# Turning the normed rows beside the attention: TensorE transposes against VectorE blocks placed by DMA

## What is computed

```python
x = x + xattn(layernorm(x), ctx, Wq, Wk, Wv, Wo)
#   q = xn @ Wq.T * 16**-0.5; k = ctx @ Wk.T; v = ctx @ Wv.T     (16 heads)
#   o = sigmoid(q k^T) v ; o @ Wo.T
x = x + ffn(layernorm(x), gate_w, Wg, Wu, Wd, Ws_g, Ws_u, Ws_d)
#   scores = softmax(h @ gate_w.T); each of 16 experts takes its top 64 rows of a batch
#   expert: (gelu(t @ Wg.T) * (t @ Wu.T)) @ Wd.T, weighted and added; shared expert on all rows
```

## Time and profile before

| | us |
|---|---|
| median of 3 runs | 1478.99 (1475.84 to 1479.41) |
| the profiled execution's own time | 1478.48 |
| its span, first to last instruction | 1476.7 |
| TensorE matmul busy | 1407.8 (95%) |
| ScalarE busy | 942.0 (64%) |
| VectorE busy | 654.3 (44%) |
| mean granted TensorE clock | 0.975 of full |

### The profile page before, as it was taken

One profiled execution on the slowest core, in us unless ns is written; L12 is line 12 of the kernel. 1 busy time (PEld: TensorE's weight loads), 2 busy tenths in 40 slices (PEclk: granted clock), 3 DMA queues, 4 the chain that ended last, 5 costly groups with the idle time before them and its releaser, 6 DMA issues.

```text
span 1476.7 us, 22519 instructions
## 1 busy us (share of the span) xinstructions
PE 1407.8 (95%) x9046; PEld 789.5 (53%) x9046; DVE 654.3 (44%) x1305; ACT 942.0 (64%) x1061; POOL 209.7 (14%) x171
## 2 busy tenths in 40 slices
PE   3897999999999999999999999999999999999996
PEld 2443434434434444443443443333788888888885
DVE  4334225325314423432632431220447677777773
ACT  0475867787787788778778778998232344334341
POOL 0000000000000000000000000020000236666664
PEclk9898999999999999999999999999899999999998
DMA  4463496286467548539647834841344446666643
GB/s 153 151 136 106 110 147 150 94 133 143 140 105 127 144 110 135 150 109 131 143 136 102 131 118 96 111 143 48 142 139 133 125 146 155 160 153 143 147 99 41
DMA packets 101145, 187.74 MB, mean 127 GB/s; under 512 B 17200, under 2 KB 51504, under 8 KB 101040
## 3 DMA queue, kind: packets, MB, share of 16 engines
q1 hardware_dynamic: 84192, 155.06, 45.4%
q0 software_dynamic: 16000, 29.91, 10.0%
q10 hardware_dynamic: 848, 1.31, 0.3%
HBM read 122.24 MB, written 64.00 MB: 126 GB/s over the span
## 4 chain that ended last, share of the span: by engine, by line
PE 89%; DMA 3%; DVE 3%; ACT 2%; issue 1%; SPq 1%; POOL 0%; POOLq 0%; DVEq 0%
PE acc L1185 26%; PE score L1225 17%; PE score L1169 17%; PE score L1240 9%; PE misc L1083 6%; PE misc L1096 6%; PE misc L1119 2%; PE misc L1104 2%; ACT probs L600 2%; PE misc L1128 1%; DMA key_scr<-key_parts 1%; PE misc L1111 1%; SPq L348 1%; DMA keys<-key_scr 1%; PE acc L1252 0%
## 5 line engine op out<-in xcount | busy, mean ns | idle before, releaser
L600 ACT ACTIVATE probs<-score 128x1024 f32<-128x1024 f32 (+1 forms) x832 | 780.8, 1048 | 207.3 <-PE score L1169 206.5
L1185 PE MATMUL acc<-probs,values 128*32 128x512 f32 (+1 forms) x3328 | 448.1, 611 | 5.7 <-ACT probs L600 3.1
L1169 PE MATMUL score<-queries,keys 48*128 48x512 f32 (+1 forms) x1664 | 317.1, 454 | 3.0 <-DMA keys<-key_scr 3.0
L1169 PEld LDWEIGHTS score<-queries,keys 48*128 48x128 f32 (+1 forms) x1664 | 127.4, 182 | 255.8 <-ACT probs L600 204.3
L609 ACT ACTIVATE gelu<-score 128x512 f32<-128x512 f32 x96 | 57.1, 595 | 214.6 <-PE score L1225 212.5
L1185 PEld LDWEIGHTS acc<-probs,values 128*32 128x32 f32 (+1 forms) x3328 | 66.4, 108 | 153.1 <-issue 131.1
L511 POOL DMA_DIRECT2D ctx_raw<-ctx_t x32 | 23.4, 732 | 810.5 <-DVE ctx_lo L686 809.4
L692 DVE CAST key_parts<-misc 128x512 fp32r<-128x512 f32 (+1 forms) x64 | 36.8, 575 | 215.8 <-PE misc L1083 201.7
L1225 PE MATMUL score<-tok_hi,gu_hi 128*128 128x512 f32 x384 | 120.1, 394 | 0.0
L1225 PE MATMUL score<-tok_lo,gu_hi 128*128 128x512 f32 x384 | 119.4, 392 | 0.0
L1225 PE MATMUL score<-tok_hi,gu_lo 128*128 128x512 f32 x384 | 119.3, 392 | 0.0
(11 more groups left out here) (128 smaller groups left out, 1457.2 us busy)
## 6 DMA issues: line engine op xcount, KB each, us to landing
keys<-key_scr SPq DMA_DIRECT2D x180, 200.2 KB, 10.2
key_scr<-key_parts SPq DMA_DIRECT2D x48, 512.0 KB, 4.5
gu_raw<-w_gu SPq DMA_DIRECT2D x17, 1024.0 KB, 6.5
ctx_raw<-ctx_t POOLq DMA_DIRECT2D x24, 512.0 KB, 4.3
queries<-query_scr SPq DMA_DIRECT2D x180, 64.0 KB, 3.0
d_raw<-w_d SPq DMA_DIRECT2D x17, 512.0 KB, 8.9
query_scr<-query_parts SPq DMA_DIRECT2D x15, 512.0 KB, 2.9
xn<-x SPq DMA_DIRECT2D x8, 512.0 KB, 3.8
```

Of the source, the lines that this page charges most:

```text
L600: act.activation(probs[0:rows, n % RING, 2 * pair:2 * pair + 2, :], score[k % 3][0:rows, :, :], ACT.Sigmoid, scale=SCALE).then_inc(probs_d ...
L1169: mm = pe.matmul(score[k % 3][0:rows, g, :], keys[quarter % KEY_RING][of, pair, P * st:P * st + rows], queries[half][of, e, pair, :], star ...
L1185: mm = pe.matmul(acc[32 * c:32 * (c + 1), :], values[b % 2][0:rows, st, half, c, :], probs[0:rows, n % RING, c, :], start=(st == 0), stop= ...
```

## The change

The T tasks of batches 1 to 7 and the N tasks of batches 0 to 6 leave the slots; each tensor is transposed in four steps instead:

1. `turn_rows` (VectorE): one instruction transposes every 32 by 32 block of the 128 x 1024 tensor into the new buffer `row_blocks`. There is one such buffer for both tensors, so a turn first waits until the placing before it has landed.
2. `place_rows` (SyncE): 16 DMAs from SBUF to SBUF, 32 partitions with two runs of 512 B each, put the blocks at their partitions, back into `norm` or `xn`. For `norm` they wait for the store of the rows (`store_norm`).
3. `split_rows` (VectorE): four instructions, cast and subtraction for each of the two halves, read SBUF and write `nt_hi` and `nt_lo`, putting the rows in order.
4. TensorE's query product waits for the split of T, its gate product for that of N (`wait_rows`).

The remaining tasks are given other slots (`at_quad`), and the slots of the layernorm pieces move by one. Some small tensors of the second stage move to its part of SBUF, which makes room for the buffer and changes no instruction.

```diff
+TURN = 32
+BLOCKS = P // TURN
+PLACE_DMAS = 16 * BLOCKS ** 2
...
-        at_quad = (12, 14, 16, 18, 20, 22, 24, 26, 28, 29, 31, 33, 35, 37, 39, 41, 43, 45, 47)
+        at_quad = (12, 14, 16, 18, 21, 23, 25, 27, 29, 34, 36, 38, 40, 42, 44, 46, 48)
     else:
-        tasks = {4: ("O", b - 1, 0), 6: ("O", b - 1, 1), 20: ("N", b - 1, 0), 21: ("N", b - 1, 1),
-                 23: ("G", b - 1)}
-        at_quad = (0, 2, 8, 10, 12, 14, 16, 18, 25, 26, 28, 30, 32, 34, 36, 38, 40, 42, 44)
+        tasks = {5: ("O", b - 1, 0), 7: ("O", b - 1, 1), 24: ("G", b - 1)}
+        at_quad = (0, 2, 10, 12, 14, 17, 19, 22, 26, 29, 31, 34, 36, 38, 41, 43, 46)
     if b + 1 < B:
-        c = b + 1
-        names = [("K", c, 0, 0), ("K", c, 1, 0), ("V", c, 0, 0), ("V", c, 0, 1),
-                 ("K", c, 0, 1), ("K", c, 1, 1), ("V", c, 1, 0), ("V", c, 1, 1),
-                 ("T", c, 0), ("T", c, 1), ("Q", c, 0), ("Q", c, 1),
-                 ("K", c, 0, 2), ("K", c, 1, 2), ("V", c, 2, 0), ("V", c, 2, 1),
-                 ("K", c, 0, 3), ("K", c, 1, 3), ("V", c, 3, 0)]
         tasks.update(zip(at_quad, names))
     return tasks
+
+
+def turn_number(kind, b):
+
+    return 2 * b + 1 if kind == "N" else 2 * b - 2
...
+            row_blocks = sa("row_blocks", [P, D // TURN, P])
...
+            def place_rows(kind, b):
+
+                i_turn = turn_number(kind, b)
+                sp.wait_ge(rows_turned, i_turn + 1)
+                if kind == "N":
+                    sp.wait_ge(post_stored, STORE * (b + 1))
+                raw = (norm if kind == "N" else xn)[:].rearrange("p t d -> p (t d)").rearrange(
+                    "p (k s) -> p k s", s=S)
+                for i in range(BLOCKS):
+                    for j in range(BLOCKS):
+                        sp.dma_start(raw[TURN * j:TURN * (j + 1), :, P * i:P * (i + 1)],
+                                     row_blocks[TURN * i:TURN * (i + 1), j::BLOCKS, :]).then_inc(rows_placed, 16)
...
-                sp.wait_ge(misc_copied, COUNT["T", b - 1, KC - 1])
+                if b == 1:
+                    sp.wait_ge(misc_copied, COUNT["T", 0, KC - 1])
+                else:
+                    sp.wait_ge(rows_split, turn_number("T", b - 1) + 1)
...
+                    sp.wait_ge(rows_split, turn_number("N", b) + 1)
...
+                    if b and q == 13:
+                        store_norm(b - 1)
+                    if b and q == 16:
+                        place_rows("N", b - 1)
+                    if b and q == 23:
+                        store_norm_t(b - 1)
+                    if b + 1 < B and q == (27 if b == 0 else 21):
+                        place_rows("T", b + 1)
+                    if b + 2 < B and q == (33 if b == 0 else 27):
+                        load_x(b + 2)
...
+            def turn_rows(kind, b):
+
+                dve.wait_ge(norm_ready if kind == "N" else xn_ready, b + 1)
+                wait_past(dve, rows_placed, PLACE_DMAS * turn_number(kind, b))
+                dve.transpose(row_blocks[:].rearrange("p j (t q) -> p t j q", q=TURN),
+                              (norm if kind == "N" else xn)[:].rearrange("p t (j q) -> p t j q", q=TURN)
+                              ).then_inc(rows_turned, 1)
+
+            def split_rows(kind, b):
+                dve.wait_ge(rows_placed, PLACE_DMAS * (turn_number(kind, b) + 1))
+                if kind == "T":
+                    wait_past(dve, nt_stored, STORE * (b - 1))
+                    if b > 1:
+                        dve.wait_ge(misc_full, COUNT["G", b - 2])
+                else:
+                    dve.wait_ge(misc_full, COUNT["Q", b + 1, 1])
+                raw = (norm if kind == "N" else xn)[:].rearrange("p t d -> p (t d)").rearrange(
+                    "p (k s) -> p k s", s=S)
+                for k in range(KC):
+                    of = raw[:, k, :].rearrange("p (i t q) -> p t i q", i=BLOCKS, q=TURN)
+                    hi = nt_hi[:, k, :].rearrange("p (t i q) -> p t i q", i=BLOCKS, q=TURN)
+                    lo = nt_lo[:, k, :].rearrange("p (t i q) -> p t i q", i=BLOCKS, q=TURN)
+                    dve.tensor_copy(hi, of).then_inc(split_step, s.up())
+                    dve.wait_ge(split_step, s.now())
+                    last = dve.tensor_tensor(lo, of, hi.bitcast(F32), ALU.subtract)
+                last.then_inc(rows_split, 1)
...
-                    if b and q == 7:
+                    if b and q == 8:
                         second_sums(b - 1)
-                    if b and q == 9:
+                    if b and q == 10:
                         norm_scale()
-                    if b and q == 11:
+                    if b and q == 12:
                         norm_apply(norm, resid, norm_ready)
+                    if b and q == 13:
+                        turn_rows("N", b - 1)
...
+                    if b and q == 22:
+                        split_rows("N", b - 1)
...
+                    if b + 1 < B and q == (26 if b == 0 else 20):
+                        turn_rows("T", b + 1)
+                    if b + 1 < B and q == (32 if b == 0 else 26):
+                        split_rows("T", b + 1)
...
+            def wait_rows(kind, b):
+                pe.wait_ge(rows_split, turn_number(kind, b) + 1)
...
+                    if b:
+                        wait_rows("T", b)
...
+                    if b < B - 1:
+                        wait_rows("N", b)
```

More of the change, by code:

```diff
@@ L75, in beside @@
 def beside(b):
+    tasks, c = {}, b + 1
+    names = [("K", c, 0, 0), ("K", c, 1, 0), ("V", c, 0, 0), ("V", c, 0, 1),
+             ("K", c, 0, 1), ("K", c, 1, 1), ("V", c, 1, 0), ("V", c, 1, 1), ("K", c, 0, 2), ("Q", c, 0),
+             ("K", c, 1, 2), ("V", c, 2, 0), ("V", c, 2, 1), ("K", c, 0, 3), ("K", c, 1, 3), ("V", c, 3, 0),
+             ("Q", c, 1)]
     if b == 0:
@@ L243, in build @@
             choice = sb("choice", [P, S])
+            row_max = sb("row_max", [P, TT * B])
+            row_sum = sb("row_sum", [P, TT * B])
+            row_inv = sb("row_inv", [P, TT * B])
+            sum4 = sb("sum4", [P, TT * B, 4])
+            sum2 = sb("sum2", [P, TT * B, 2])
+            top_w = sb("top_w", [P, 2, CAP])
+            top_i = sb("top_i", [P, CAP], U32)
+            top_row = sb("top_row", [P, 2, CAP])
         score = [keep.enter_context(nc.psum_tensor(f"score{i}", [P, 2, S], F32)) for i in range(3)]
@@ L264, in build @@
         norm_ready = sem("norm_ready")
+        rows_turned = sem("rows_turned")
+        rows_placed = sem("rows_placed")
+        rows_split = sem("rows_split")
         split_step = sem("split_step")
@@ L390, in store_norm_t @@
             def store_norm_t(b):
-                sp.wait_ge(misc_copied, COUNT["N", b, KC - 1])
+                if b == B - 1:
+                    sp.wait_ge(misc_copied, COUNT["N", b, KC - 1])
+                else:
+                    sp.wait_ge(rows_split, turn_number("N", b) + 1)
                 for part, tile in enumerate((nt_hi, nt_lo)):
@@ L429, in _ @@
                                 stack_queries(task[1], 0)
-                        elif task[0] == "T" and task[2] == KC - 1 and task[1] + 1 < B:
-                            load_x(task[1] + 1)
-                        elif task == ("N", b - 1, 0):
-                            store_norm(b - 1)
-                        elif task == ("N", b - 1, 1):
-                            store_norm_t(b - 1)
                         elif task == ("G", b - 1):
```

8 lines of the change are left out of this document (removed).

## The result

The changed kernel takes **1530.69 us** (median of 4 runs, 1527.72 to 1532.59) against 1477.63; the ratio is 1.036 (95% interval 1.033 to 1.038). The forecast said slower, 1490.5, with a range to 1508: the sign was right, the size was not, and the range missed it by 23 us.

The account below looks back on a forecast made before the run. TensorE was taken as the bound. Transposes -15.3, batch ends -2.1, batch 0 -7.3, VectorE waits +28.3, batch 7 +3.8, clock +4.5 sum to +11.9 on 1478.48; median 0.5 higher: 1490.5 us, range 1470 to 1508.

Parts of the forecast that it names:

- What goes, and the slots: TensorE, batches 0 to 6: 26 transpose tasks gone, -15.3 us; last task at quad 46, -2.1 us over six batches.
- The idle time at the start of batch 1: TensorE's 3.04 us wait for key reads would go, covered by a later-placed quad and query product.
- batch 0 and this start: More cover for the key-copy and key-read waits, and no clock fall behind: -7.3 us, besides batch 0's transposes.
- VectorE's pieces: Turn 1.30 us and split 2.36 hold TensorE at quads 15, 24 and 28: 4.72 us per batch, +28.3 in six.
- Rival 3: VectorE's pieces fit without holding TensorE, so the kernel is faster: 1462 us; chance 0.18, shared with both kinds of luck.
- 16 issues per tensor at 5.43 / 12 = 0.45 us ... cost 0: SyncE's placings take 7.2 us per tensor, land in 3.0, and hold up nothing in batches with products for cover.
- The spare time: Slack between the end of T's turn, after N's placing, and VectorE's next needed copy (quad 22): 1.1 us.
- Rival 1: Placing lands late and holds VectorE's copy of quad 22 and all behind it: 1504 us, or 1536; chance 0.15.
- its rule of 7 us per microsecond: Each microsecond of placing beyond the spare 1.1 us costs 7 us in all; 1.9 late makes 13.
- 3.8 forecast: Batch 7, no products for cover: gate product waits for N's placing and split, +3.8 us.
- With a wait of 1.9 us just ahead of it I expect all seven: 3 x 1.5: TensorE's clock falls behind the gate product in all seven windows instead of four: +4.5 us.

Follow-up runs that it names:

- e3: Changed kernel with turn, placing and split of both tensors left out, so products read what lies in the buffers; 1460.33 us, ratio 0.989 to the kernel before.
- e5: Changed kernel with only VectorE's order changed: N's turn and T's split behind the read-outs, N's split ahead of quad 22's copy; 1492.87 us, ratio 1.010.
- e9: Changed kernel with 6 of the 24 matmuls of each gate product, all waits kept; 1507.11 us, ratio 1.019.
- e15: Changed kernel with the gate product in two tasks of 12 matmuls, in quads 24 and 25; 1540.57 us, ratio 1.043.
- e1: Changed kernel without the 16 placing DMAs per tensor, each tensor with its own block buffer, rows left in wrong places; 1502.21 us, ratio 1.017.
- e2: Changed kernel with a block buffer and semaphore for each tensor, so T's turn doesn't wait for N's placing; 1513.25 us, ratio 1.024.
- e6: Changed kernel with the placing DMAs issued from GpSimd's queue instead of SyncE's; 1515.09 us, ratio 1.025.
- e8: Changed kernel with the VectorE order of e5 and placing through HBM (four writes and one read per tensor); 1464.58 us, ratio 0.991.
- e12: e8 with the first query product in quad 30 instead of 29 and the next key product in 32 instead of 31; 1459.90 us, ratio 0.989.
- e11: e8 with the gate product in two tasks of 12 matmuls, in quads 24 and 25; 1452.11 us, ratio 0.983.
- e13: The edits of e11 and e12 together (gate product in halves, later query product); 1449.20 us, ratio 0.983.
- e14: Kernel before, transposes still on TensorE, with the gate product in halves in quads 23 and 24; 1474.88 us, ratio 0.9986.
- e4: Kernel before with the change's slots for all tasks, the transposes still on TensorE; 1480.97 us, ratio 1.002.

## Why the prediction was wrong

**What goes, and the slots: right.** 2.7 us per batch forecast, 2.5 measured (e3 against batches without a fall). The idle time at the start of batch 1 is gone, as forecast. For batch 0 and this start 8.5 us were put down (7.3 and two transposes). Batch 0 gained 4.1, and some 2.9 more lie in batch 1, which before took 125.2 us where other batches with one short fall took 122.3: 7 us together. The rest is the long wait: one quad more of cover would have left 9.47 - 1.66 = 7.8 us of it, which e5, e9 and e15 show (7.67), but the profiled execution of the change had 9.94.

**VectorE's pieces: right.** Turn 1.25 (1.30 forecast), split 2.2 (2.36), waits 0.50, 1.55 (with the placing out of the way) and 2.14 (less the 0.30 that was there) against 0.74, 1.86 and 2.12. e5 shows that the order of the queue makes them. The rule that I weighed here, 311 ns for a block turn of 128x128 in bf16 in the Trainium skill ("VectorE: DVE Perf Modes", "The three transpose paths"), would have made 2.5 us; for a float32 tensor of eight such blocks in one instruction the trace shows half of that, and the row nearest in kind (1.23 us for a subtraction of the same size) was the better guide. Rival 3 is out.

**"16 issues per tensor at 5.43 / 12 = 0.45 us ... cost 0": the step that failed first.** The issues took 0.69 each. The price came from a row of another shape (queries, 16 partitions with runs of 2 KB) and had no upper end; I had put the doubt into the landing, which was faster than taken (1.9). The spare time was 1.1 us and the issues alone took 3.9 more; with the store 0.6 later and the landing shorter, N was in place at 26.8 instead of 24.0, 1.7 us past what was spare, and the gate wait grew by 1.8 us in the mean. Rival 1 was right in its place and its sign, T's turn waiting for a DMA, but not in its reason, a slow landing; and its rule of 7 us per microsecond held too little: 12 us for these 1.7, where e1 gives 28. Of these some 11 are the wait in batches 1 to 6, 4 the clock there, 10 batch 7 and 4 batch 0, which varies by itself. In batch 7, with nothing to cover it, the gate waits 4.84 us (3.8 forecast) and the clock is at half for 13.7 us behind it.

**"With a wait of 1.9 us just ahead of it I expect all seven: 3 x 1.5": the term that was mis-sized most.** Right in direction, but with the forecast's own waits (e1) the clock is at half speed twice per batch, 6.8 or 10.2 us behind the gate and 3.4 or 6.8 behind the wait at quad 28. A batch without falls and with those waits would be 118.3 + 0.5 + 1.6 + 2.1 = 122.5 us; it took 127.9 in the mean. That is 5.4 us per batch for falls, 32 us in six batches, where 1.5 per batch were allowed. I priced a fall by the shortest row (4.81 us for two quads) and took each wait as costing its own length. In the change as it stands the same sum leaves 6 us per batch.

**The 40 us that were missing,** by the profiled executions: batches 1 to 6 of e1 are together some 21 us longer than the forecast had them (120.8 - 2.7 + 4.7 + 1.5 = 124.3 us each), nearly all of it the clock; the late placing adds 15 to them; batch 7 has 4 more than the 3.8 and the one short fall put down for it; batch 0 and the start of batch 1 gained 1.5 less. The stage behind the attention, which the change doesn't touch, took 2 us less.

**What stays open.** How long a fall lasts after a given wait varied from batch to batch within one run: behind the same 1.55 us before the gate product it was 6.8 us in four batches of e1 and 10.2 in two. These runs don't say why, nor whether the fall at quad 28 needs the one before it.

## What to carry to other kernels

A queue of DMAs is paid per issue: count issues of the shape in question, bound them from above too, and where an operation waits on the last of them, prefer few large ones, even through HBM. On an in-order engine put new work behind the piece that the bounding engine waits for: the same instructions cost 53 us in one order and placing and gained 28 in another (with the gate product halved). A buffer shared by two tensors makes one's lateness the other's: a second one (e2) took some 15 us back in batches 1 to 6. And where TensorE bounds, price a new wait with the half-speed time behind it, not by its own length.

## What the runs showed of the hardware

- A block turn of a 128x1024 float32 tensor takes VectorE 1.25 us as one instruction, with a four-dimensional pattern.
- Casts and subtractions that read and write SBUF in pieces of 32 elements keep their speed: 0.42 and 0.69 us for 128x512.
- SBUF to SBUF placings of 32 partitions with two runs of 512 B: median 0.60 us of SyncE's queue, 0.64 to 0.71 in the mean of 16 for N (0.54 of GpSimd's, e6), 1.9 us to land.
- TensorE's granted clock fell behind waits of 1.6 us that were followed by 24 narrow matmuls (e1, e2), in four to seven batches of seven behind 24 narrow matmuls without any wait (the kernel before, e3, e8, e12), and not behind 12 narrow ones between full quads (e11, e13, e14). It fell at waits of 2.1 us with full quads behind them, 3 to 7 us after an earlier fall (the change, e1), and not at waits of 1.15 us with full quads behind them (e4). Where a wait came first, halving the product made the time at half speed longer, 13.7 us against 10.2 (e15).
